# Half-row loads issued at the head of each half, and SyncE's program put into the loop of the key and value stage

## The reference, cut to what matters

```
row_zero = x.sum(-1) == 0
q_exp = where(row_zero[..., None], 0, cond[:, None, :])
self_feat = concat([x, q_exp], -1) @ W_self.T + b_self
for d in range(2):                                  # adj, or adj transposed
    A = (adj if d == 0 else swap(adj))[:, :, :20, :]
    kv = self_feat[:, :20]
    qh = self_feat @ Wq[d].T + bq[d];  kh = kv @ Wk[d].T + bk[d]
    aff = where(A.sum(-1) > 0, qh . kh / sqrt(32), NEG) + A @ w_bias + b_bias
    w = softmax(aff)
    output += (w @ kv) . Wout[d] + bout[d]
return x + relu(self_feat + output)
```

## Time and profile before

| what | us |
|---|---|
| median of three runs | 1922.33 |
| the profiled execution, its own time | 1922.33 |
| its span in the profile | 1920.5 |
| TensorE matmul busy in the span | 1892.6 (99%) |
| VectorE, ScalarE, GpSimd busy | 1306.0, 576.4, 835.3 |
| mean granted clock of TensorE, as a share of full | 0.995 |

### The profile page before, as it was taken

The page is one execution under the profiler, slowest core; times in us unless marked ns, Lnnn a source line. Parts: engine busy times, 40 slices in busy tenths (PEclk is TensorE's granted clock), DMA queues, the critical chain, the costliest instruction groups (busy, mean ns, idle before and its releaser), DMA issues.

```text
span 1920.5 us, 34076 instructions
## 1 busy us (share of the span) xinstructions
PE 1892.6 (99%) x11020; PEld 1651.4 (86%) x11020; DVE 1306.0 (68%) x1897; ACT 576.4 (30%) x1189; POOL 835.3 (43%) x746
## 2 busy tenths in 40 slices
PE   8799999999999999999999999999999999999999
PEld 6799999888888888888888888888888888888887
DVE  2533332377777777777777777777777777777776
ACT  2323322233333333333333333333333333333332
POOL 0232231254444444444444444444444444444442
PEclk9899999999999999999999999999999999999999
DMA  4223322464444444444444444444444444444431
GB/s 159 76 80 92 97 87 80 124 145 121 121 120 121 120 120 120 120 120 120 120 120 120 120 120 120 120 120 120 120 120 120 120 120 120 120 120 120 120 99 62
DMA packets 227950, 219.86 MB, mean 114 GB/s; under 512 B 58176, under 2 KB 179008, under 8 KB 223808
## 3 DMA queue, kind: packets, MB, share of 16 engines
q1 hardware_dynamic: 223440, 219.24, 41.7%
q10 hardware_dynamic: 4464, 0.02, 0.1%
HBM read 164.39 MB, written 54.79 MB: 114 GB/s over the span
## 4 chain that ended last, share of the span: by engine, by line
PE 78%; DVE 1%; DMA 1%; issue 0%; POOL 0%; ACT 0%; ACTq 0%; SPq 0%; DVEq 0%
PE bank L1486 36%; PE bank L1434 19%; PE bank L1422 12%; PE bank L1458 7%; PE bank L1447 4%; DMA adj<-in_mask_BxSxSx_ik 1%; PE bank L1407 0%; DVE nodes_t L88 0%; DVE qt_main L1245 0%; PE bank L1495 0%; DVE res L1232 0%; DVE sc L1209 0%; DVE res L1230 0%; DVE nodes_t L1181 0%; POOL rc L1120 0%
## 5 line engine op out<-in xcount | busy, mean ns | idle before, releaser
L1120 POOL TENSOR_TENSOR rc<-nzb,cqg 128x512 f32<-128x512 bf16 x256 | 265.1, 1041 | 413.2 <-DVE qt_main L1245 413.2
L1422 PEld LDWEIGHTS bank<-kbd,qt_main 128*128 128x128 f32 x2048 | 243.5, 192 | 19.5 <-DVE sc L1209 13.4
L1245 DVE SCALAR_TENSOR_TENSOR qt_main<-bank,bq_all,rc 128x512 f32<-128x512 f32 x256 | 189.6, 741 | 91.8 <-PE bank L1486 86.6
L1098 POOL TENSOR_TENSOR sc<-sc,mx 128x640 f32<-128x640 f32 x128 | 163.3, 1276 | 199.0 <-DVE mx L1214 199.0
L1422 PE MATMUL bank<-kbd,qt_main 128*128 128x80 f32 x2048 | 247.5, 274 | 0.2
L1332 ACT ACTIVATE wtt<-bank 128x384 f32<-128x384 f32 (+1 forms) x256 | 111.1, 435 | 381.7 <-PE bank L1447 381.6
L1220 DVE TENSOR_REDUCE sm<-sc 128x32 f32<-128x640 f32 x128 | 104.7, 818 | 162.7 <-ACT sc L1324 162.7
L1486 PE MATMUL bank<-nodes_h,wq_h 128*128 128x512 f32 x512 | 210.3, 411 | 1.3 <-DVE qt_main L1245 1.3
L1486 PE MATMUL bank<-xh_odd,wq_h 128*128 128x512 f32 x512 | 210.5, 411 | 0.0
L1486 PE MATMUL bank<-xh_odd,wq_l 128*128 128x512 f32 x512 | 202.3, 395 | 0.0
L1486 PE MATMUL bank<-nodes_h,wq_l 128*128 128x512 f32 x512 | 202.2, 395 | 0.0
(11 more groups left out here) (126 smaller groups left out, 3825.8 us busy)
## 6 DMA issues: line engine op xcount, KB each, us to landing
rows<-in_x SPq DMA_DIRECT2D x128, 256.0 KB, 5.0
xk<-in_x SPq DMA_DIRECT2D x32, 1024.0 KB, 5.9
res<-c_dram SPq DMA_DIRECT2D x32, 1024.0 KB, 4.5
out<-res SPq DMA_DIRECT2D x128, 256.0 KB, 2.1
adj<-in_mask_BxSxSx_ik SPq DMA_DIRECT2D x32, 440.0 KB, 5.5
adj<-in_mask_BxSxSx_ik SPq DMA_DIRECT2D x128, 110.0 KB
k_dram<-kv_kst SPq DMA_DIRECT2D x64, 160.0 KB, 1.8
v_dram<-kv_vt SPq DMA_DIRECT2D x256, 40.0 KB
```

The lines of the kernel that those rows point to most:

```text
L1098: pool.tensor_tensor(s, s, mx[:, b % 2, :].unsqueeze(2).to_broadcast([P, DIRS * H, NG]), ALU.subtract).then_inc(s_shifted, 1)
L1120: pool.tensor_tensor(rc[:, c % 2, :].rearrange("p (b n) -> p b n", b=G), nzb[:, par, :].rearrange("p (b n) -> p b n", b=G), cqg[:, par, c, ...
L1245: nc.vector.scalar_tensor_tensor(out=qt[:, c, :], in0=bank[c % 2][:], scalar=bq_all[:, c:c + 1], in1=rc[:, c % 2, :], op0=ALU.add, op1=ALU ...
L1422: mm = nc.tensor.matmul(dst, qt[:, c, b * N:b * N + N], kbd[:, c, :, b * NG:b * NG + NG], start=True, stop=True)
```

## The change

SyncE's stream now goes through `halves` as the other engines' do, so its two middle blocks (halves 2 to 5) are a loop on the chip, with addresses and semaphore counts from registers. Within a half the order is changed as well: the load comes first, ahead of the key stores. At the head of half n SyncE waits until the rows of half n have been turned, and loads half n + 2 into their buffer; in half 6 it loads the first rows of the main loop there. The number of loads and stores is the same.

```
-            def one_half(n, par):
+            def one_half(blk, n, par, first, last, tail):
+                if not tail:
+                    sp.wait_ge(x_turned, C * (n + 1))
+                    load_half_rows(sp, v, n + 2, par, loaded[par])
+                elif not last:
+                    sp.wait_ge(x_turned, C * HALVES)
+                    load_group_rows(sp, v, 0, main_loaded)
                 for p in range(NK):
                     sp.wait_ge(kv_out, 2 * NK * n + p + 1)
                     sp.dma_start(v["k_dram"][p, :, bass.ds(n * HB, HB), :], ...)
-                if n + 3 < HALVES:
-                    sp.wait_ge(x_turned, C * (n + 2))
-                    load_half_rows(sp, v, n + 3, 1 - par, loaded[1 - par])
-                elif n + 2 == HALVES:
-                    sp.wait_ge(x_turned, C * HALVES)
-                    load_group_rows(sp, v, 0, main_loaded)
                 for m in range(NK):
                     d, c = m // C, m % C
                     sp.wait_ge(v_turned, NK * n + m + 1)
                     ...
-            sp.wait_ge(x_turned, C)
-            load_half_rows(sp, v, 2, 0, loaded[0])
-            for n in range(HALVES):
-                one_half(n, n % 2)
+            halves(sp, one_half)
```

## The result

The changed kernel takes 1941.97 us (median of 6 runs, 1936.33 to 1943.08) against 1921.87 us before: a ratio of 1.0096, 95% interval 1.008 to 1.0113. In a second set of four runs it took 1938.05 us against 1922.00, ratio 1.0084 (1.0067 to 1.0101). It is slower by 16 to 20 us, clear of the 0.3% that can be told from no change. The profiled execution took 1937.90 us, 15.6 more than the profiled one before, with a span of 1936.1.

A forecast was written before the change was run, and what follows sets the result against it. TensorE, busy for 1892.6 of 1920.5 us, was taken to bound the kernel. Gaps of 9.1 us and 5.1 us of lowered clock made 14.2 us, added to 1922.3 for 1936.5 us; range 1925 to 1944 us.

The forecast's parts named there:

- The chain and its slack: Key and value stage: late rows delay VectorE's turn, ScalarE's cast and key output, then TensorE; no gap up to 208.9 us.
- P4 at T + 1.8: TensorE's P4 matmuls start 1.8 us after T, the time at which VectorE can start the turn of the rows.
- VectorE's waits of some 8 us in half 1 and 11 in halves 3 to 5: Profile sign: VectorE's turn of rows waits this long for the rows' DMA, where it waited nothing before.
- the two links: TensorE waits for ScalarE's key output of P1, then more weakly for VectorE's zero flags at T + 3.2, needed at T + 3.6.
- The gaps: TensorE idle in halves 1 to 5 of the key and value stage: 0, 0.5, 2.7, 3.2, 2.7; 9.1 us in sum.
- rival C: Looped half-row issues pay registers in full, 0.74 us not 0.66; value groups 2.11: 19.6 us more, 1942 us; chance 0.14.
- The comparison with the main loop's row loads: Main loop's heavier row loads took 2.08 and 2.02 us, no difference looped, so looped half-row issues were given 0.66 us.
- The clock: TensorE's clock falls behind three gaps longer than 2.0 us, 1.7 us lost each: 5.1 us more.
- Rival B: Gaps on TensorE without the clock's fall: 9.1 us more, 1931.4 us; chance 0.15.
- Rival D: Register work hidden in SyncE's looped value stores, below 0.41 us per store: gaps of 1.8 us, 1924 us; chance 0.16.
- Rival E: The change doesn't reach TensorE, as issue time is small or the slack longer than counted: 1922 us; chance 0.05.
- The sum: TensorE's gaps of 9.1 us and its clock's fall of 5.1 us: 14.2 us more, 1936.5 us; chance 0.48.

The follow-up runs named there:

- experiment 3: Changed kernel, but ScalarE takes out the keys of P0 and P1 before its first cast of rows: 1935.13 us, ratio 1.0059.
- experiment 4: Changed kernel with ScalarE's keys of P0 and P1 ahead of its first cast and VectorE's zero flags ahead of the turn: 1921.57 us, ratio 0.9996.
- experiment 8: Changed kernel again, unaltered: 1938.05 us in four runs, then three single traced executions of 1939.38, 1938.13 and 1937.88 us.
- experiment 6: Changed kernel, but a half's rows in the second stage are loaded by 16 DMAs of 40 KB, not 8 of 80 KB: 1975.54 us, ratio 1.0269.
- experiment 5: Changed kernel, but a half's rows in the second stage are loaded by 4 DMAs of 160 KB, not 8 of 80 KB: 1926.53 us, ratio 1.0019.

## Why the prediction was right

**The chain and its slack** were right. P4 at T + 1.8 was measured as T + 1.72 to 1.83; VectorE's waits of some 8 us in half 1 and 11 in halves 3 to 5 are 8.4, and 12.1, 11.6 and 11.4. Experiments 3 and 4 show that key output and zero flags are the two links, in this order and 0.2 to 0.4 us apart.

**The gaps** were forecast as 0, 0.5, 2.7, 3.2 and 2.7, 9.1 in sum, and measured as 0, 1.00, 3.52, 3.16 and 2.78, 10.5 in sum. Two terms of that sum were mis-sized. The looped load issues were given 0.66 us and took 0.78 from start to start ((6.01 - 0.58) / 7), a little above rival C's 0.74. The comparison with the main loop's row loads misled. There the DMA's own instruction is shorter in the loop (0.35 us for 0.49), which makes up for nearly all of the register work: 0.53 to 0.56 us from start to start for 0.49 to 0.53. Here it is 580 ns against 602 written out, so only 22 ns are hidden. The difference to the forecast is 7 x 0.12 = 0.8 us in each of four halves. In the other direction, the looped value stores of halves 3 and 4 took 15.3 and 15.5 us for 32 where 15.9 was counted; those of half 2 took 16.0. So half 2 and half 3 came out longer, and in halves 4 and 5 the two errors nearly cancel.

**The clock** was forecast at 1.7 us for each gap above 2 us, 5.1 in sum, and cost 6.2 in the profile after, since one stretch at half clock was longer; in the trace of experiment 8, and in two of the three behind it, each of the three stretches was short, as forecast. Rival B (no fall) is out. Rival D (registers hidden in the value stores) is out: 0.48 to 0.50 us a store, above its point of 0.41 (its four gaps add up to 1.7 us and not 1.8, which changes nothing). Rival E is out: eight issues take 6.0 us and the last lands 2.4 us after its start, and experiment 6, which moves the same bytes with twice the issues, is 34 to 37 us slower than the changed kernel. The Trainium skill's rule that the time to start a DMA is usually small relative to the DMA itself (DMA: Bandwidth & Descriptors, "Issuing engines are not separate DMA queues") doesn't help here: a single issue is 0.6 to 0.8 us against 2.4, but the eight of a load add up.

**The sum** of 14.2 us compares with 15.6 in the profiled execution. The median of the first six runs was 20.1 us above before and that of the other four 16.1. What lies above 16 us comes with the longer executions, of which there is no trace. So it is luck that rival C's 1942 meets the first median of 1941.97: C's price of a load issue was near, but its value stores (2.11 us a group) took 1.9 to 2.0, and the five traced executions, of 1937.31 to 1939.38 us, lost 15 to 17 us and not its 19.6.

## What to carry to other kernels

SyncE is an engine with a schedule: its issues here cost 0.38 to 0.80 us each, and hardly less when they move less of the same tensor. A load that stands behind 32 small stores starts only when all of them have been issued. Before moving a load, or turning a queue's program into a loop, find the slack between the landing and the first instruction that the bound engine needs, count every issue against it, and look on the engines between for work that stands behind the late one without needing it. Two changes that are each free can exceed the slack together, so a result of no difference says nothing about how near the edge is.

## What the runs showed of the hardware

- The price of an issue hardly depended on its size: 40, 80 and 160 KB of the same rows cost 0.77, 0.78 and 0.80 us from start to start in a loop (12.1 us for 16, 6.0 for 8, 3.0 for 4) and 0.64 to 0.66 written out (10.19, 5.11 and 2.57 us). It does depend on what is moved: a value store, also of 40 KB, cost 0.38 written out.
- Register work ahead of a DMA (37 + 29 ns and the gaps around them) raised the price of a half-row load from 0.64 to 0.78 us and that of a value store from 0.38 to 0.48. For the row loads of the main loop it was some 0.03 us (0.49 to 0.53 written out, 0.53 to 0.56 looped), since the DMA's own instruction became shorter there (0.49 to 0.35 us). Why one kind hides it and the other doesn't is not shown.
- The fall of TensorE's clock to 1.2 GHz behind an idle time is not certain at a given length. It came behind 2.78 and 3.5 us in the changed kernel and 2.82 and 3.08 in experiment 3, and did not behind 2.54 there, 1.56 in experiment 5 and 1.00. Behind 2.3 us at the same place of the program it came in the trace before and not in the trace after; in `prepare_weights` it came behind 2.0 us in the trace before and not behind 2.25 in the trace after.
- Jumping back at the end of SyncE's loop took 0.3 us from the branch to the next instruction in the changed kernel (246.9 to 247.2) and 2.5 us once, in experiment 6 (268.2 to 270.8).
